# Two-stage attention and soft-routing kernel: halves for every fourth routing tile, and a new order at two ends

## What is computed

```
q, k, v = (gelu(x @ W1 + b1) @ W2 + b2) for each of q, k, v
scores  = (q @ k.T) / scale * tril(ones)
x1      = layernorm(x + layernorm(scores @ v) * ln_w + ln_b)

xn       = layernorm(x1) * ln_gamma + ln_beta
logits   = (xn / |xn|) * scale @ (mu / |mu|)          # 256 columns: 16 experts x 16 slots
dispatch = softmax(logits over the tokens)
combine  = softmax(logits over the 256 slots)
slot_in  = dispatch.T @ xn                            # the "fold"
slot_out = gelu(slot_in @ w1 + b1) @ w2 + b2
out      = layernorm(x1 + combine @ slot_out)
```

## Time and profile before

| | us |
|---|---|
| median of three runs | 590.03 |
| the profiled execution | 590.34 |
| its span in the trace | 588.6 |
| PE busy | 572.5 |
| DVE busy | 485.6 |
| ACT busy | 393.4 |
| POOL busy | 393.9 |

### The profile page before, as it was taken

How to read it: one execution, slowest core, us unless ns; L and a number is a source line. 1 busy time by engine, 2 the same in 40 slices (tenths; PEclk the granted TensorE clock), 3 DMA queues, 4 the chain that set the end, 5 groups by cost and what they waited for, 6 DMA issues and landing times. The chain is left out here.

```text
span 588.6 us, 11698 instructions
## 1 busy us (share of the span) xinstructions
PE 572.5 (97%) x3796; PEld 528.0 (90%) x3796; DVE 485.6 (83%) x1048; ACT 393.4 (67%) x855; POOL 393.9 (67%) x395
## 2 busy tenths in 40 slices
PE   9999999999999999999999999979999999999994
PEld 7889989999999999999998999968999999888883
DVE  6579889899898898888989989979988777557885
ACT  4765666676766667667677666567688777435765
POOL 0869779789797797787977978785646443104453
PEclk9999999999999999999999999999999999999998
DMA  8324134043141331422403403105555555923445
GB/s 234 81 73 108 22 87 99 12 107 43 65 107 18 89 71 41 102 33 74 107 13 94 86 23 74 26 11 98 84 72 72 73 73 73 147 33 108 143 144 179
DMA packets 163473, 47.04 MB, mean 80 GB/s; under 512 B 139470, under 2 KB 159340, under 8 KB 163436
## 3 DMA queue, kind: packets, MB, share of 16 engines
q1 hardware_dynamic: 163424, 46.57, 36.9%
q10 hardware_dynamic: 12, 0.00, 0.0%
HBM read 21.39 MB, written 8.39 MB: 51 GB/s over the span
## 5 line engine op out<-in xcount | busy, mean ns | idle before, releaser
L523 POOL TENSOR_TENSOR h_lo<-xn_all,h_hi 128x512 fp32r<-128x512 f32 x32 | 41.4, 1295 | 68.2 <-ACT xn_all L649 67.1
L647 ACT ACTIVATE h_hi<-bank,bias_col 128x512 fp32r<-128x512 f32 x96 | 66.4, 692 | 18.8 <-PE bank L793 17.1
L791 PE MATMUL bank<-xnT_hi,w_hi 128*128 128x512 f32 x188 | 76.2, 405 | 0.0
L792 PE MATMUL bank<-xnT_lo,w_hi 128*128 128x512 f32 x188 | 74.4, 396 | 0.0
L793 PE MATMUL bank<-xnT_hi,w_lo 128*128 128x512 f32 x188 | 74.2, 395 | 0.0
L682 ACT CAST state_hi<-bank 128x512 fp32r<-128x512 f32 x57 | 33.5, 588 | 50.1 <-PE bank L926 50.1
L1608 PE MATMUL bank<-xn_all,e_tok 128*128 128x257 f32 x256 | 65.1, 379 | 0.0
L1190 DVE TENSOR_TENSOR state_lo<-bank,state_hi 128x512 fp32r<-128x512 f32 x57 | 39.4, 691 | 29.0 <-ACT state_hi L682 29.0
L1686 PE MATMUL bank<-w_sb,ET_all 128*128 128x256 f32 x256 | 55.4, 379 | 0.0
L1686 PEld LDWEIGHTS bank<-w_sb,ET_all 128*128 128x128 f32 x256 | 48.6, 190 | 6.6
L1507 ACT ACTIVATE e_tok<-bank,shift,xinv 128x256 f32<-128x256 f32 x64 | 36.1, 565 | 27.3 <-PE bank L1598 20.5
(11 more groups left out here) (202 smaller groups left out, 2081.6 us busy)
## 6 DMA issues: line engine op xcount, KB each, us to landing
x_all<-in_L_attn_x SPq DMA_DIRECT2D x16, 512.0 KB, 3.9
kT<-k_turn SPq DMA_DIRECT2D x128, 64.0 KB, 2.5
ET_all<-e_turn SPq DMA_DIRECT2D x64, 128.0 KB, 3.8
xn_all<-in_xT SPq DMA_DIRECT2D x15, 512.0 KB, 4.7
out<-xn_all SPq DMA_DIRECT2D x15, 512.0 KB, 3.0
w_sb<-in_L_ffn_w SPq DMA_DIRECT2D x2, 512.0 KB, 5.3
xn_all<-in_L_ffn_w SPq DMA_DIRECT2D x2, 512.0 KB, 6.6
xn_all<-in_xT SPq DMA_DIRECT2D x2, 256.0 KB, 3.5
```

The costliest lines, as they stand in the source:

```text
L523: pool.tensor_tensor(h_lo[:, V_SLOT, m, :], hv[:, m, :], h_hi[:, V_SLOT, m, :].bitcast(F32), ALU.subtract).then_inc(hv_split, 1)
L647: nc.scalar.activation(h_hi[:, h_slot(j, n), m, :], ps, ACT.Gelu, bias=bias(n, m))
L791: nc.tensor.matmul(ps, w[0], xs[0], start=start, stop=False, skip_group_check=shared)
L792: nc.tensor.matmul(ps, w[0], xs[1], start=False, stop=False, skip_group_check=shared)
```

## The change

Three things, of which the diff shows the core. Lines of the changed kernel are some 3 to 60 higher than those before.

First, in the routing, the fourth tile of each group (`FOLD_AT`) is folded by six f32r products in place of the two f32 matmuls. ACT rounds its exponentials to `fold_e_hi`, POOL makes `fold_e_lo` and both halves of its tokens. The other three tiles keep f32 matmuls, now 258 columns wide.

Second, at the end of the attention: `divide_tokens` goes from POOL to ACT, as four instructions; `weight_tokens` and the inversion of group 0's norms go behind the halves that PE waits for. DVE makes all three `v_sum` earlier and two `add_out` later.

Third, at the end of the kernel: DVE sums the first tile of the next group while it waits for POOL's residual, DVE norms tile 0 of the last group, and ACT sends out the first pair itself. In the diff stand, in this order, POOL's body and ACT's new function in the attention, then POOL, ACT and PE in the routing, and DVE at the end.

```diff
                 def body(g, j, ba, attend=True, project=True, settle=True, more=True):
                     if not project:
                         split_vsum(a, 1)
+                        invert_norms(pool, 0, 0, minus_half[:, :])
+                        weight_tokens(1)
                         add_beta(pool, 1, 1)
                         return
...
-                    if not more:
-                        divide_tokens(1, 1)
-                        weight_tokens(1)
                     split_ktok(g, 0)
+                    if attend:
+                        invert_o(pool, a, 1)
...
+                def divide_tokens(k, q, tiles):
+                    for t in tiles:
+                        tile = GT * k + t
+                        nc.scalar.activation(xn[q][:, t, 0:D], x1_all[:, tile, :], ACT.Copy,
+                                             scale=r2_all[:, tile:tile + 1]).then_inc(tok_divided, 1)
...
                     for q in range(GB):
+                        split_fold_xn(GB * b + q, q)
+                        split_fold_e(GB * b + q)
...
+                def split_fold_e(k):
+                    pool.wait_ge(fold_e_rounded, k + 1)
+                    pool.tensor_tensor(fold_e_lo[:, :], e_tok[:, FOLD_AT, :], fold_e_hi[:, :].bitcast(F32), ALU.subtract
+                                       ).then_inc(fold_e_split, 1)
...
                     exps(b, t)
+                    if t % GT == FOLD_AT:
+                        act.wait_ge(e_ready, TB * b + t + 3)
+                        nc.scalar.copy(fold_e_hi[:, :], e_tok[:, FOLD_AT, :]).then_inc(fold_e_rounded, 1)
...
+                    if t % GT == FOLD_AT:
+                        pe.wait_ge(fold_xn_split, GB * b + q + 1)
+                        pe.wait_ge(fold_e_split, GB * b + q + 1)
...
+                            nc.tensor.matmul(ps, fold_e_hi[:, part], fold_xn_hi[:, :], start=False, stop=False)
+                            nc.tensor.matmul(ps, fold_e_hi[:, part], fold_xn_lo[:, :], start=False, stop=False)
+                            last = nc.tensor.matmul(ps, fold_e_lo[:, part], fold_xn_hi[:, :], start=False,
+                                                    stop=(t == TB - 1))
...
                         if pair == 1:
+                            sum_y(k + 1, (0,))
                             dve.wait_ge(y_added, k + 1)
```

More of the change, by code:

```diff
@@ L224, in add_beta @@
         def add_beta(engine, k, q):
-            engine.wait_ge(tok_scaled, GT * k + GT)
+            if k == 1:
+                engine.wait_ge(tok_weighted, 1)
+            else:
+                engine.wait_ge(tok_scaled, GT if k == 0 else GT * k)
             engine.tensor_tensor(xn[q][:, :, 0:D], xn[q][:, :, 0:D],
@@ L376, in build @@
             tok_divided = asem("tok_divided")
+            tok_weighted = asem("tok_weighted")
             vsum_rounded = asem("vsum_rounded")
@@ L617, in body @@
                         split_mu()
-                    if not more:
-                        invert_norms(pool, 0, 0, minus_half[:, :])
                 run_groups(body, pool, lambda: None)
@@ L772, in body @@
                     round_ktok(g)
+                    if not more:
+                        divide_tokens(1, 1, (0, 1))
                     round_v(g, 0)
+                    if not more:
+                        divide_tokens(1, 1, (2,))
                     round_v(g, 1)
@@ L1269, in body @@
                             sum_v(g, j, 0)
+                            sum_v(g, j, 1)
+                            sum_v(g, j, 2)
+                            return
                         add_out(dve, a, 2)
                         add_out(dve, a, 3)
-                        if not more:
-                            return
                         z_summed(dve, a, 1)
@@ L1431, in _ @@
                     sp.dma_start(out_t[:, GT * k:GT * k + GT, :], y[k % GB][:, :, 0:D]).then_inc(stored[k % GB], 16)
[L1432 to L1436 removed]
+                sp.wait_ge(last_normed, 3)
+                sp.dma_start(out_t[:, GT * LAST + 2:GT * LAST + 4, :], y[LAST % GB][:, 2:4, 0:D]
+                             ).then_inc(stored[LAST % GB], 16)
                 for q in range(GB):
@@ L1579, in _ @@
                 act.wait_ge(y_shift, LAST + 1)
-                for t in range(2):
-                    yt = y[LAST % GB][:, t, 0:D]
-                    nc.scalar.activation(yt, yt, ACT.Identity, scale=rs_y[:, LAST % 2, t:t + 1],
-                                         bias=nm_y[:, LAST % 2, t:t + 1]).then_inc(y_normed, 1)
+                yt = y[LAST % GB][:, 1, 0:D]
+                nc.scalar.activation(yt, yt, ACT.Identity, scale=rs_y[:, LAST % 2, 1:2],
+                                     bias=nm_y[:, LAST % 2, 1:2]).then_inc(y_normed, 1)
+                act.wait_ge(last_normed, 1)
+                act.wait_ge(y_normed, GT * LAST + 1)
+                act.dma_start(out_t[:, GT * LAST:GT * LAST + 2, :], y[LAST % GB][:, 0:2, 0:D]
+                              ).then_inc(stored[LAST % GB], 16)
             @block.tensor
```

89 lines of the change are left out of this document (55 added, 34 removed).

## The result

The kernel after takes 600.54 us, the median of five runs (600.01 to 601.56), against 590.40 for the kernel before beside it (589.85 to 590.80): the ratio is 1.0177, with a 95% interval of 1.0162 to 1.0192. It is slower by 10.1 us. The profiled execution took 601.56 us with a span of 599.8; before, the span was 588.6. The 11.2 us between the spans lie here: 0.4 ahead of the last call of the attention, where nothing was changed; 1.2 in that call and the barrier; 9.6 in the routing; 0.0 in the experts and the mixing; 0.0 behind PE's last product.

The account below looks back on a forecast made before the run. PE was taken to bound the routing before, a closed loop of ACT and POOL after. Routing +7.1, attention's end -0.3, kernel's end -0.5 make +6.3 us: 596.3 against the median of 590.03; 8-in-10 range 591.0 to 600.0.

Parts of the forecast that it names:

- the closed loop of ACT and POOL: Routing: ACT's next exponential waits for POOL's power, queued behind a subtraction that waits for ACT's copy; routing +7.1 us.
- A cheaper fold: Routing, PE: six products at 0.12 us, a group needs 7.05 instead of 7.20; net gain at most 2.1 us.
- The turn: Routing: one turn of ACT and POOL takes 7.08 us undisturbed, 7.40 disturbed; 11 turns of 7.40, 2 of 7.08.
- two open hand-overs: Routing loop: the two hand-overs besides POOL to ACT, estimated at 0.08 us together, bounds 0 and 0.24.
- strict exclusion: Routing: POOL's subtraction waits for a whole running scale_tokens instruction, up to 0.4 us, not 0.18; sum up to 2.4 higher.
- Extra lengths: Routing, added to the turns: copy_slots 1.6 us, apply_z 3.0, POOL's two z chains 1.4; together 6.0.
- The cast: Routing, POOL's cast for the token halves: priced at 0.65 us without a row, bounds 0.3 and 1.3.
- Last group: Routing: from group 15's first exponential to the routing's end 5.6 us, with the last half coming at 4.9.
- The attention's end: Last attention call and barrier: PE's next update some 0.5 us earlier; 0.3 us gain, bounds gain 1.8 and loss 0.5.
- The kernel's end: Kernel's end: DVE's last chain starts 0.4 us earlier, last transfer not behind the first pair's; gain 0.5, bounds 0.9 and 0.
- rival (4): Routing: loop longer, by strict exclusion or a cast near 1.3 us; 599 to 601 us; chance 0.06 shared with another rival.

Follow-up runs that it names:

- e1: The kernel after, with POOL's group power (invert_norms) ahead of the subtraction of the exponentials' low half instead of behind it: 594.80 us, ratio 1.0081.
- e5: The kernel after, with one more ACT copy of the fourth tile's exponentials, which nothing reads, ahead of the copy POOL waits for: 606.00 us, ratio 1.0267.
- e6: The kernel after, with the products with the low halves left out of every fourth tile's fold, the halves still made and waited for: 600.66 us, ratio 1.0185.
- e9: e2 with POOL's power ahead of the subtraction and each of the two z and x1 chains cut in two, invert_x1 a turn later: 590.49 us, ratio 1.0006.
- e7: The kernel after, with DVE's four scale_tokens moved one tile earlier in the turn, away from POOL's subtraction and power: 601.89 us, ratio 1.0189.
- e3: The kernel before with the reordered end of the attention alone: 591.16 us, ratio 1.0015.
- e13: e9's fold with e3's attention end, state 1's low half ahead of floor_norms, and 12 unread products in each gap that e12 fills: 589.70 us, ratio 0.9991.
- e12: e3 with unread products on PE: 18 ahead of its wait for state update 1, 12 behind its last attention product: 591.08 us, ratio 1.0009.
- e8: e3 with DVE's order of before (neither the two v_sum nor the two add_out moved): 592.10 us, ratio 1.0035.
- e2: The kernel before with the fold change alone, the attention's end and the kernel's end as before: 599.95 us, ratio 1.0163.
- e14: e4 with the transfer of the first pair of the last group's tiles back on SP instead of ACT: 590.59 us, ratio 0.9999.
- e4: The kernel before with the changed order and the ACT transfer at the kernel's end alone: 590.51 us, ratio 1.0009.
- e10: e9 with the logits ahead of the fold at a batch's last tile too, as at every other tile: 590.34 us, ratio 0.9999.

## Why the prediction was wrong in size and right in kind

The forecast was 596.3 us, with a range to 600.0; the kernel takes 600.5. Direction and mechanism were right: the closed loop of ACT and POOL is where +7.1 was put and +9.6 found, and e1, e5 and e6 show it, one by opening it, one by lengthening it, one by taking away PE's work, which leaves the loop as it is. In the spans the miss is 4.9 us: 2.5 in the routing, 1.5 in the attention's end, 0.5 at the end, 0.4 in a part that was not changed.

- **A cheaper fold.** Right. Six products start 0.12 us apart (524.38, 524.49, 524.62), and with PE as the bound a turn is 7.06 (e1), predicted 7.05. But the kernel before did not have 7.20 in all turns, and the waits for the last half (0.33) and at batch ends use the gain up: e9 is no faster than before.
- **The turn.** Forecast 7.40, measured 7.55. (The terms as listed give 7.06 for the undisturbed turn, not 7.08, and 7.39 for the disturbed one.) No term was far off: the fourth exponential to the copy 0.70 for 0.69, the copy and its hand-over 0.48 for 0.42, the subtraction 0.86 for 0.81, the power and its hand-over 1.32 for 1.29, the rest 4.19 for 4.18. Five shortfalls of 0.01 to 0.06 make 0.15, and that counts twelve times: 1.8 us. One more turn than foreseen was disturbed (0.3). These 2.1 of the 2.5 us are the step that failed in the routing. My two open hand-overs had bounds of 0 and 0.24, and I took 0.08; they measured 0.12. The strict exclusion, by which the subtraction would have waited for a whole `scale_tokens` instruction, didn't come: 0.18 was added and 0.17 measured (0.90 for the 0.73 of e7).
- **Extra lengths.** 6.0 forecast, 5.7 measured. The cast, priced at 0.65, takes 0.40, and up to 0.68 where DVE's `scale_tokens` run beside it.
- **Last group.** 5.6 forecast, 6.3 measured: the last half came 5.34 us behind the exponential and not 4.9.
- **The attention's end.** Forecast -0.3, measured +1.2 in this trace and +1.0 by e3. The failed step is the sentence that PE's next update starts some 0.5 us earlier. I let three `v_sum` be held by POOL and forgot the instruction between them and the state half: `floor_norms`, which I would have priced at some 0.15. It took 1.23 and cost 1.1 (e13 against e12). The block's end moved with it: POOL's addition, forecast to end at 395.8 (the listed terms give 395.4), ended at 397.74, since the weighting waited for ACT's last divide until 393.24, and DVE's four `scale_tokens` ended at 399.20 and not at 397.3. The second failure is that the clock has no term here: I kept it for the routing's idle pieces, where it stayed at 1.00, and didn't ask for it in the attention. The idle time of 2.87 us brought it down in three of six profiled executions that have this wait.
- **The kernel's end.** Forecast -0.5, measured 0. DVE's last norm does end earlier, 3.69 us behind PE's last product for 3.97 before. I priced the issue of the last transfer and took its duration as fixed; the landing didn't follow it. My lower bound of 0 is what came; the reason I gave for it, that the transfers share what they wait for, was not tested.
- **The range.** The top, 600.0, lies 0.5 below the measured time. All errors but one have one sign. The worst bounds of the attention's end and of the kernel's end, +0.8 and +0.5 on the forecast, reach 597.6; the rest was in a sum of small hand-overs and in the last group, to which I gave no width of their own. That rival (4), 599 to 601, holds the measured time is luck: neither the strict exclusion nor a cast near 1.3 us came.

## What to carry to other kernels

Before an instruction that waits for another engine is put into an in-order queue, ask what stands behind it: here a power that had been ready for 1.7 us was queued behind a subtraction, and the swap of two lines was worth 5.7 us, where 5.7 us less of TensorE's busy time (e6) shortened the routing by 1.0 in the trace and the median not at all. When a loop of engines becomes the bound, price each hand-over from a row and give their sum a width, since every error counts once per turn. And when TensorE is made to finish early ahead of a fixed barrier, look at the granted clock behind the gap before counting the gain.

## What was not expected of the hardware

A DVE instruction of four columns with one SBUF input (`floor_norms`, `TENSOR_SCALAR`) took 1.23 us while POOL made pass after pass, 0.37 in e8 at another moment, and 0.17 where POOL is quiet. Its neighbours with two SBUF inputs were held in the same way.

Behind an idle time of PE of 2.1 to 2.9 us the clock fell in some executions and not in others. The same code of the attention with the same wait of 2.87 to 2.89 us had its clock at half behind it in the kernel after, e3 and e6 and at full in e1, e5 and e7; a wait of 2.43 to 2.46 us left it up in the kernel before, e2 and e14 and brought it to 0.68 in e4, 0.73 in e9 and 0.62 in e10 (stretch 386 to 389 us). Behind the wait of 2.87 the fall cost 0.7 to 1.1 us of the length in the table, behind the wait of 2.43 at most 0.3 (13.80 in e4, 13.77 in e9, 14.14 in e10, for 13.80); in the first turn of the routing it cost 0.8 to 1.6. In e2, e5 and e10 it fell behind the routing's last fold (0.50 in e2 from 526 to 528 us), and from there to PE's last product they took 68.5 us where all others took 66.9; their profiled executions, 601.79, 607.77 and 592.31, lie 1.8 to 2.0 us above their medians, most of it by this. The page TensorE: Matmul & The Clock Gate of the Trainium skill says in Part 1 that the clock is released by activity and varies from run to run for one kernel; these runs agree as to the latter.

POOL's instructions beside DVE's `scale_tokens` were stretched, not stopped: the subtraction from 0.73 to 0.90, the power from 1.01 to 1.20, the cast from 0.40 to 0.62 (e1, 426.20). The subtraction at 494.19 in the kernel after began while an instruction of DVE had 0.32 us left, and took 0.17 longer. DVE's own instruction of 0.47 was held for up to 2.33 us by a pass of 2.2 (e12).
